# A 12-layer transformer kernel on one core: start-up loads, normalisation on ScalarE, a planner's slack and two deeper rings

## The reference, cut to what matters

```
x = _layernorm(x + _L0_attn_ref(x, ...))       # rotary self-attention
x = _layernorm(x + _L0_xattn_ref(x, ctx, ...)) # causal attention, context attention, two gained norms, linear
x = _layernorm(x + _L0_ffn_ref(x, ...))        # int8-style quantised linear layer
x = _layernorm(x + _L1_attn_ref(x, ...))       # self-attention mixed with a local band
x = _layernorm(x + _L1_xattn_ref(x, ctx, ...)) # context attention with a given mask
x = _layernorm(x + _L1_ffn_ref(x, ...))        # 1 of 8 experts
x = _layernorm(x + _L2_attn_ref(x, enc, scorer_logits, ...)) # causal attention, scorer attention, GELU MLP
x = _layernorm(x + _L2_xattn_ref(x, ctx, ...))
x = _layernorm(x + _L2_ffn_ref(x, ...))        # 2 of 16 experts
x = _layernorm(x + _L3_attn_ref(x, ...))       # attention over the four sequences
x = _layernorm(x + _L3_xattn_ref(x, ctx, ...))
x = _layernorm(x + _L3_ffn_ref(x, ...))        # 3 of 31 experts plus a shared one
```

## Time and profile before

| | us |
|---|---|
| median of 3 runs | 2639.15 |
| lowest and highest run | 2636.06 and 2651.93 |
| the profiled execution | 2615.75 |
| its span from the first to the last instruction | 2613.9 |

### The profile page before, as it was taken

How to read it: one execution, slowest core, us unless ns; L and a number is a source line. 1 busy time by engine, 2 the same in 40 slices (tenths; PEclk the granted TensorE clock), 3 DMA queues, 4 the chain that set the end, 5 groups by cost and what they waited for, 6 DMA issues and landing times. The chain is left out here.

```text
span 2613.9 us, 43617 instructions
## 1 busy us (share of the span) xinstructions
PE 2080.8 (80%) x15046; PEld 1028.6 (39%) x15046; DVE 1549.0 (59%) x3259; ACT 1145.6 (44%) x2217; POOL 770.5 (29%) x943
## 2 busy tenths in 40 slices
PE   3799999987799999668999898864958776795373
PEld 1123355543333344554554444434922222333252
DVE  5678766657878843365665555342567776437134
ACT  0267765562177765122654766631423221161031
POOL 4201102113411101333112112115406667203663
PEclk9779999988799999677997998976978887796576
DMA  3410011110111000342011001005910000100265
GB/s 124 167 57 26 26 39 32 27 28 1 49 34 29 20 17 14 106 160 61 26 33 32 20 12 31 24 36 179 326 39 0 1 0 0 43 16 18 78 188 150
DMA packets 135005, 148.44 MB, mean 57 GB/s; under 512 B 29366, under 2 KB 119926, under 8 KB 133635
## 3 DMA queue, kind: packets, MB, share of 16 engines
q1 hardware_dynamic: 97604, 104.58, 13.8%
q10 hardware_dynamic: 29376, 24.97, 3.1%
q0 software_dynamic: 7808, 16.10, 1.7%
HBM read 72.61 MB, written 26.99 MB: 38 GB/s over the span
## 5 line engine op out<-in xcount | busy, mean ns | idle before, releaser
L1538 DVE TENSOR_REDUCE maxima<-psM 128x2 f32<-128x1024 f32 (+4 forms) x640 | 677.6, 1080 | 343.9 <-PE psM L1209 135.5
L1402 ACT ACTIVATE probs<-psE 128x512 f32<-128x512 f32 (+2 forms) x1248 | 698.8, 584 | 397.8 <-PE psE L1232 188.3
L1232 PE MATMUL psE<-q_stack,k_stack 53*128 53x512 bf16 (+3 forms) x1152 | 371.8, 360 | 43.8 <-ACT probs L1402 34.1
L1209 PE MATMUL psM<-k_stack,q_stack 51*128 51x512 bf16 (+3 forms) x1280 | 350.8, 349 | 8.7 <-DVE maxima L1538 6.9
L1686 POOL TENSOR_SCALAR pool_t<-mean_var 128x4 f32<-128x4 f32 x60 | 15.0, 251 | 655.0 <-DVE mean_var L1463 651.3
L1232 PEld LDWEIGHTS psE<-q_stack,k_stack 53*128 53x128 bf16 x1152 | 98.0, 94 | 242.6 <-ACT probs L1402 160.7
L2237 POOL DMA_INDIRECT by_token<-probs,y_slot x148 | 141.7, 957 | 130.8 <-DVEq L2181 121.0
L1209 PEld LDWEIGHTS psM<-k_stack,q_stack 51*128 51x128 bf16 x1280 | 101.5, 97 | 163.7 <-issue 86.2
L2013 ACT COPY probs<-psE 128x128 f32<-128x128 f32 x148 | 39.4, 266 | 282.0 <-PE psE L1942 176.6
L1143 PE MATMUL psM<-masks_bf,ident_bf 64*128 64x128 bf16 (+2 forms) x832 | 153.1, 266 | 5.1 <-DMA k_stack<-k_parts 4.9
L1252 PE MATMUL psB<-probs,values 128*32 128x256 f32 (+3 forms) x1728 | 154.8, 430 | 1.7 <-ACT probs L1402 1.2
(11 more groups left out here) (475 smaller groups left out, 3805.2 us busy)
## 6 DMA issues: line engine op xcount, KB each, us to landing
q_stack<-q_parts SPq DMA_DIRECT2D x432, 64.0 KB
values<-experts_dram SPq DMA_DIRECT2D x40, 514.0 KB
values<-experts_dram SPq DMA_DIRECT2D x79, 128.5 KB, 2.1
k_stack<-k_parts SPq DMA_DIRECT2D x156, 64.0 KB
hid<-experts_dram SPq DMA_DIRECT2D x15, 514.0 KB
work<-experts_dram SPq DMA_DIRECT2D x15, 514.0 KB
sorted<-hid ACTq DMA_DIRECT2D x7, 1024.0 KB, 10.7
c_values<-sorted ACTq DMA_DIRECT2D x78, 65.0 KB
```

Of the source, the lines that this page charges most:

```text
L1209: out, len(heads), keys, lo, max_mask(c, t), lambda i, to, start, stop: nc.tensor.matmul(to, q_stack[lo:lo + R_MAX, job.a % Q_SLOTS, pair_ ...
L1232: lambda h, to, start, stop: nc.tensor.matmul(to, ks[lo:lo + R_END, pairs[h], k * P:k * P + c.kn], q_stack[lo:lo + R_END, job.a % Q_SLOTS, ...
L1402: nc.scalar.activation(probs[0:c.kn, m % 2, heads[0]:heads[-1] + 1, q0:S], psE[0:c.kn, n % 2, 0:len(heads) * (S - q0)].rearrange("p (h q) ...
L1538: nc.vector.tensor_reduce(top, psM[:, at:at + len(banks), 0:per * keys].rearrange("p b (h k) -> p b h k", h=per), AX_X, ALU.max, negate=Tr ...
```

## The change

Six things change together.

1. `pack` is put in another order, with what the first job needs in the first 2327 columns; only these are loaded in start-up, and the other 6968 columns by a DMA from ACT's queue at the end of start-up. PE waits for it (`pack_loaded`) before its first `q`, `k`, `v` or `out` that does not belong to the first attention.
2. The row constants are laid over 128 partitions (22 numbers each), so that their casts and subtractions are 128x22; the moves of halves and rows go from SP's queue to ACT's. The memsets of the q and k stacks write pairs of bf16 ones as one f32 number, and the large ones are in another order; `probs` is cleared before the wait for the loads.
3. Normalisation moves from DVE to ACT: the new task `post_n` (and `post_c`) does four activations Identity(root * x + shift), with shift = -mean * root from two more POOL instructions at the end of `root`. Gain, shift and residual stay on DVE in `post_b`, which now exists only for "twice" and "tail" jobs and waits for ACT.
4. The planner adds 0.5 us of slack to the readiness of PE's small tasks, where what they wait for is on another engine, and has new lengths for the moved tasks.
5. The order of the sequences in segment 2 goes from 0 1 2 3, 0 1 2 3, 1 0 2 3 to 0 1 2 3, 1 0 2 3, 0 1 2 3.
6. `Y_SLOTS` goes from 3 to 5.

```diff
-    [("ident", P), ("rot", P), ("cos", S), ("sin", S), ("band", len(BAND) * P)]
-    + [(f"{n}_{w}", D) for n in ("L0a", "L0s", "L0c", "L1a", "L1c", "L2s", "L2c", "L2x", "L3c")
+    [("ident", P), ("rot", P), ("cos", S), ("sin", S)] + [(f"L0a_{w}", D) for w in ("wq", "wk", "wv", "wo")]
...
+FIRST_W = PACK_AT["L0s_wq"][0]
+TWO_ONES = 1.0 + 0x3F80 / 2.0 ** 23
...
+SLACK = {("PE", task) for task in ("q", "k", "v", "rq", "rk", "rows", "gather", "local", "turn", "out", "back", "hidden")}
...
-        self.put(t + 4.0, "post_b", job)
+        self.put(t + 3.6, "post_n", job)
+        if job.post in ("twice", "tail"):
+            self.put(t + 4.6, "post_b", job)
...
-            return short.get(task, 2.0 if task == "gelu" else 0.6)
+            return short.get(task, {"gelu": 2.0, "post_n": 1.25, "post_c": 1.25}.get(task, 0.6))
         if engine == "POOL":
-            return 2.8 if task == "root" else 1.3 if task == "k_split" and not x.att.wide else 3.8
+            return 3.2 if task == "root" else 1.3 if task == "k_split" and not x.att.wide else 3.8
...
-                begin_at[engine, item] = max([ended[a] + hop(a[0], engine) for a in after[engine, item]], default=0.0)
+                slack = 0.5 if (engine, item[0]) in SLACK else 0.0
+                begin_at[engine, item] = max([ended[a] + hop(a[0], engine) + (slack if a[0] not in ("ISSUED", engine) else 0.0)
+                                              for a in after[engine, item]], default=0.0)
...
-                sp.dma_start(pack[:], io["pack"]).then_inc(loads, 16)
+                sp.dma_start(pack[:, 0:FIRST_W], io["pack"][:, 0:FIRST_W]).then_inc(loads, 16)
...
-                sp.wait_ge(cast, 4)
+                sp.wait_ge(cast, 3)
...
-                sp.wait_ge(halves_cast, 2)
-                for both in (ident_bf, masks_bf):
-                    for lo in (0, 64):
-                        sp.dma_start(both[lo:lo + 64, 1, :], both[64 - lo:128 - lo, 0, :]).then_inc(rolled, 16)
-                sp.wait_ge(row_parts, 1)
-                sp.dma_start(rows[1:2, :], row_mid).then_inc(rolled, 16)
-                sp.dma_start(rows[2:3, :], row_low).then_inc(rolled, 16)
-                sp.wait_ge(rolled, 16 * 6)
...
                 nc.gpsimd.memset(zeros_bf[:], 0.0).then_inc(cast, 1)
+                nc.gpsimd.memset(k_stack[:].rearrange("p k h n -> p (k h n)").bitcast(F32), TWO_ONES).then_inc(cast, 1)
+                nc.gpsimd.memset(kc_stack[:], 1.0).then_inc(cast, 1)
+                nc.gpsimd.memset(c_values[:], 0.0).then_inc(cast, 1)
+                nc.gpsimd.memset(q_stack[:].rearrange("p s h n -> p (s h n)").bitcast(F32), TWO_ONES).then_inc(cast, 1)
                 nc.gpsimd.memset(hid[:], 0.0)
-                nc.gpsimd.memset(k_stack[:], 1.0).then_inc(cast, 1)
...
             def _(act):
                 act.wait_ge(loads, 16 * 12)
+                act.wait_ge(halves_cast, 2)
+                for both in (ident_bf, masks_bf):
+                    for lo in (0, 64):
+                        act.dma_start(both[lo:lo + 64, 1, :], both[64 - lo:128 - lo, 0, :]).then_inc(rolled, 16)
+                act.wait_ge(row_parts, 1)
+                for n, part in enumerate((row_high, row_mid, row_low)):
+                    act.dma_start(rows[n:n + 1, :].rearrange("o (p w) -> o p w", p=P), part).then_inc(rolled, 16)
+                act.wait_ge(rolled, 16 * 7)
+                nc.scalar.dma_start(pack[:, FIRST_W:PACK_W], io["pack"][:, FIRST_W:PACK_W]).then_inc(pack_loaded, 16)
...
                 nc.vector.memset(values[:], 1.0)
+                nc.vector.memset(probs[:], 0.0)
...
-                me.mark(nc.vector.tensor_copy(rows[0:1, :], row_f))
+                me.mark(nc.vector.tensor_copy(row_high, row_f))
...
-                nc.vector.memset(probs[:], 0.0)
...
+                        if rest and task in ("q", "k", "v", "out") and not (job.att and job.att.rope):
+                            pe.wait_ge(pack_loaded, 16)
+                            rest = False
...
+                        elif task in ("post_n", "post_c"):
+                            u, part = job.u, 1 if job.kind == "quantized" or task == "post_c" else 0
+                            src = yt if task == "post_c" else {"norm": xt, "inner": hres, "inner2": hres}.get(job.post, yt)
+                            to = xt if task == "post_c" or job.post in ("std", "mlp") else yt
+                            act.wait_ge(root_done, plan.roots[job, part] + 1)
+                            for t in range(QT):
+                                last = nc.scalar.activation(to[:, u, t, :], src[:, u, t, :], ACT.Identity,
+                                                            bias=shifts[:, u, t:t + 1], scale=roots[:, u, t:t + 1])
+                            last.then_inc(normed, 1)
...
-                    def normalise(job, part, out, src):
...
-                        dve.wait_ge(root_done, plan.roots[job, part] + 1)
...
                         elif task == "post_b":
                             u = job.u
-                            part = 1 if job.kind == "quantized" else 0
-                            src = {"norm": xt, "inner": hres, "inner2": hres}.get(job.post, yt)
-                            to = xt if job.post in ("std", "mlp") else yt
-                            normalise(job, part, to[:, u], src[:, u])
+                            dve.wait_ge(normed, turned_no["post_n", job])
...
-                            nc.gpsimd.tensor_tensor(y, y, t, ALU.mult).then_inc(root_done, 1)
+                            me.mark(nc.gpsimd.tensor_tensor(y, y, t, ALU.mult))
+                            me.wait()
+                            me.mark(nc.gpsimd.tensor_tensor(t, mean_var[:, u, :, 0], y, ALU.mult))
+                            me.wait()
+                            nc.gpsimd.tensor_scalar(shifts[:, u, :], t, -1.0, None, ALU.mult).then_inc(root_done, 1)
...
-            W_SLOTS, X_SLOTS, Y_SLOTS = 5, 7, 3
+            W_SLOTS, X_SLOTS, Y_SLOTS = 5, 7, 5
...
-        ] for u in range(B)], [0, 1, 2, 3, 0, 1, 2, 3, 1, 0, 2, 3]), linear)
+        ] for u in range(B)], [0, 1, 2, 3, 1, 0, 2, 3, 0, 1, 2, 3]), linear)
```

83 lines of the change are left out of this document (43 added, 40 removed).

## The result

The changed kernel takes 2690.7 us (median of 4 runs, 2681.8 to 2695.1) against 2637.6 us for the kernel before (4 runs, 2633.2 to 2652.0): ratio 1.0195, 95% interval 1.0159 to 1.0232. That is 53 us slower, where 2611 was forecast and 2634 was the top of the range.

What follows compares the result with a forecast made beforehand. No engine bounds it throughout: PE from 200 to 320 us, DVE from 560 to 720. Terms -17.0 - 11 + 7.7 - 5 - 2 = -27.3 us gave 2588.4 from 2615.75, stated as median 2611, range 2584 to 2634.

Steps and rivals of the forecast that it cites:

- Start-up, -17.0: Start of the kernel: smaller first load and rows over 128 partitions; PE starts at 23.5 instead of 40.5 us, -17.0 us.
- the -13 taken from the rule: Start-up's weaker end: casts queue behind POOL's memsets, as two-port DVE casts and GpSimd exclude each other; -13 us.
- Normalisation on ACT, -11: Quantised-job stretch of segment 1, 560 to 720 us: relieving DVE of normalisation saves 11 us, ends 0 and -19.
- the first rival: Stretch in segment 1 gives nothing, its chains taking over from DVE: -16.3 us in all, median 2623; chance 0.20.
- Root and fills at the ends, +7.7: Segment ends and two segment starts: two more POOL instructions per root and more fills cost 7.7 us.
- a rival with -25: Clock is won: the new order keeps PE busy in half of the half-rate time, -25 us, median 2586; chance 0.20.
- half clock was to come only at the ends: Rival at the segment ends: fills take twice as long, +31.8 us in all, median 2644; chance 0.05.
- the sign of a wrong forecast: Forecast is wrong if granted clock in segment 1's first 120 us, or at 1200 and 1380, differs from before.
- Rings, -7: Expert stages 3 and 2: less excess POOL idle time and fewer slot waits, -5 and -2 us.
- The order of the sequences: Segment 2: the new order moves which chain is tight, not the work; 0 us, with +-5.
- ACT as head of the line: Where PE waits for probabilities, normalisations and root waits on ACT hold up exps: +43 us, median 2682; chance 0.05.

Runs made afterwards that it cites:

- e14: The changed kernel with a slack of 0.4 us instead of 0.5; ratio 0.9966 to the kernel before.
- e11: The changed kernel without slack and with normalisation on DVE, so start-up, five slots and sequence order alone; ratio 0.9973 to the kernel before.
- e7: The changed kernel with slack kept for the order but not in the rule that places PE's fills; ratio 1.0176 to the kernel before.
- e2: The changed kernel with normalisation back on DVE, slack kept; ratio 1.0020 to the kernel before.
- e3: The kernel before with the 0.5 us slack alone added; ratio 1.0145 to the kernel before.
- e5: The changed kernel run once more, nothing edited; ratio 1.0195 to the kernel before.
- e6: The changed kernel with one fill per tile on PE in expert stage 3; ratio 1.0193 to the kernel before.
- e9: The changed kernel with 21 needless register loads in SyncE's stream in expert stage 3; ratio 1.0249 to the kernel before.
- e8: The changed kernel with gaps filled down to 0.1 us instead of 0.3; ratio 1.0181 to the kernel before.
- e15: The changed kernel with a slack of 0.6 us instead of 0.5; ratio 1.0096 to the kernel before.
- e1: The changed kernel without the 0.5 us slack, all else as changed; ratio 0.9967 to the kernel before.
- e4: The kernel before with normalisation on ACT alone, including the two added root steps; ratio 1.0032 to the kernel before.
- e13: The kernel before, nothing edited, run for a profile on the same chip as e14, e15 and e16; 2618.2 us, one run.
- e16: The changed kernel without slack, the same kernel as e1, run again on the chip of e13, e14 and e15; ratio 0.9946 to the kernel before.
- e10: The kernel of e1 with 21 needless register loads in SyncE's stream in expert stage 3; ratio 0.9989 to the kernel before.

## Why the prediction was wrong

**Start-up, -17.0: right, -16.1.** PE began at 24.35 for 23.5, the row steps took 0.17 to 0.18 us each, and the rest of the pack was covered. The first cast took 3.04 us beside POOL's memsets, 1.5 more than before; the two-port rule of the Trainium skill (SBUF — State Buffer, Who interferes with whom) agrees with that row. It cost start-up nothing: in e14 the same cast began 1.5 us later and ended at the same 16.4 us, so the -13 taken from the rule was too dear. Some of the gain comes back behind it: e11's segment 1 is 4 us longer than before's.

**Normalisation on ACT, -11: wrong in sign.** The stretch that was to shrink, from the first to the last clamp of the quantised jobs of segment 1 (L1753 before), is 72.0 and 71.7 us in the two traces of before, and 72.3 to 78.8 in twelve of the thirteen traces with ACT normalising (e7, with its own rule for fills, took 92.5). With DVE normalising and slack it is 65.0, in e2 and e3: like to like, the move made this stretch 1 to 5 us longer without slack and 10 to 14 with 0.5. DVE was relieved in it by 15 us in the window of 160 us, as foreseen (115 busy for 130, 576 to 736 us; 19 were named). It was not what the stretch waited for. That was the first rival (0 instead of -11), and it was still too kind: a normalisation takes 1.65 us on ACT where my estimate from the earlier trace rows was 1.15 (those two activations read psM, these read SBUF; whether that is the reason was not tested), and the root has two steps more. In the part with segment 3, where single chains stand open, the length is 555 to 569 us in all 13 traces with ACT and 549 to 553 in all 7 with DVE: +11 between the means, where I had 2.7 for one end and one start. Of the 11, 7 are loss to half clock and 4 are rest: the added steps cost about what I had, and the clock that falls meanwhile, for which I had nothing, costs more. By itself the step measured +0.3% (-0.1 to +0.7). The rule of the Trainium skill cited against the move (Perfetto Trace Analysis, Optimizing Scalar/DVE Operations) was right in direction, and the trace agrees: 1.65 us on ScalarE, 1.11 on DVE. No row says in which mode DVE ran.

**Root and fills at the ends, +7.7: right there, wrong in reach.** The last step of segment 3 is 0.65 us later, as worked out (0.6 to 0.8). But this was the only term in which the slack had a price. Inside the segments it had none, and there slack alone costs 28 us in segment 1 and 12 in segment 2 (e3). In the changed kernel 10 and 14 us of it are rest, and e7 takes 9 and 11 of these away by placing the fills without the slack: fills in the way of work. This is the step that failed first: I had counted 59 more fills in the order and costed only those at the three ends.

**The clock: the step that failed most.** I gave it a rival with -25 and none with +25; half clock was to come only at the ends. It was lost where I did not look: 31 us in segment 1, 23 of them behind the quantised jobs, 11 in segment 2, 6 with segment 3. In the 90 us behind the last quantising instruction 6.5 to 8 us are lost in the five traces with DVE and no slack, 14 in the five with ACT and no slack, 9 and 15 in the two with DVE and slack, and 28 to 36 in the changed kernel, e5, e6 and e9, whose plans of segment 1 are the same. With other fills or another slack beside ACT it is 19, 13, 10 and 13 (e7, e8, e14, e15). So ACT has a share that repeats in each of these plans, and the large loss belongs to this one plan.

What I had named as the sign of a wrong forecast looked elsewhere: in the first 120 us of segment 1 the clock is 0.70 and 0.76 in the two traces of before and 0.67 and 0.72 in those of the changed kernel, with 28 and 29 us lost; the dip 40 us into segment 2 is still there (0.50, then 0.55 and 0.62); and the one at 1380 is gone, 1.00 for 0.5. With slack 0.4 segment 2 lost 52 us instead of 71. No count of instructions told which stretches fall; a term of 0 with a range of both signs, some +-40 us, would have been honest.

**Rings, -7: right in kind, more than sized where it shows.** In the five traces with SyncE at its pace stage 3 takes 133 to 135 us with five slots and 143 to 145 with three: -10 for -5, all of the excess and not half; stage 2 -1 to -2 for -2. Where SyncE is slow, DVE's 38.6 us of slot waits become waits for weights. That the slots bring nothing there is likely and not shown, since no kernel with three slots was profiled there. **The order of the sequences** was not tested apart.

**The rival "ACT as head of the line"** gave 2682, near the measured 2691, by a mechanism that the runs refuse in that size: it put 70 us on the path, alone the move costs 0.3% (7 us), and with slack 0.4 instead of 0.5 the same work on ACT ends at 0.9966. A number that fits is no support for its story. What stays open is why a slack of 0.4 costs nothing where 0.5 and 0.6 cost 45 to 50 us, and why normalisation on ACT loses time to half clock in each of these plans.

## What to carry to other kernels

Where a planner orders the work, price an edit of its rules by a band of at least the scatter between neighbouring settings (here some 1.9% for 0.1 us of slack), and try two neighbours before believing either. Compare stages by two numbers, time lost to half clock and the rest: the busy share shows neither. Spread the issues of a bulk transfer where they stand in the queue of an engine that the critical one waits for; that was worth 23 us here, more than start-up's 16. Moving them to another queue was not tried.

## What the hardware showed

**The clock can stay at half with PE busy throughout.** From 743 to 776 us the profile shows PE busy without a gap, and the granted clock was 0.51, the lower of the two levels. The Trainium skill (TensorE: Matmul & The Clock Gate, Part 1: The HAM clock gate) has the rate come back once PE has been busy. These rows do not agree: 33 us of unbroken busy time did not bring it back, nor 34 in e5. They show busy time by instructions, and no row here says how much of the array was at work.

**SyncE's pace differed between chips.** On two chips, those of e1 to e4 and e13 to e16, all eight executions profiled (the kernel before among them) had 11 to 14 SyncE instructions over 0.5 us from the start of expert stage 3 on, most of them behind the last weight, and the kernel before had a median of 2622 us on both. On three others, and where the changed kernel ran first, all eleven profiled had 49 to 82 (counted from 20 us before the stage), stage 3 took 158 to 162 us, and the kernel before had medians of 2634 to 2641. No identical code was profiled on both sorts, so the chip as cause is strongly suggested and not shown; e1 and e10, alike but for the pad, are the nearest pair: 2281 and 2275 us in the segments, 134 and 161 in stage 3. The Trainium skill (Runtime: NRT & Kernel Launch, Instruction fetch mechanics) has an engine's instructions fetched ahead at a cost mostly hidden; if these pauses are fetches, the trace does not agree, but no row says what they are. A difference of two traces from different chips is not safe, and cost me 16 us of false lead. A ratio against a kernel run beside it is safer, but two such ratios from different chips are not safe to compare either: the kernel before differs by 12 to 19 us between the sorts, and those with five slots by 26 in stage 3.
